# Soft mixture of experts: the weights are multiplied with gelu's vectors first, and with two experts' W2 after

## The reference

```python
dispatch = softmax(logits, over the rows n)                    # per slot
combine  = softmax(logits, over all 16 * 128 slots)            # per row
slot_in  = einsum('bnd,bnes->besd', x_ln, dispatch)
h        = gelu(einsum('besd,edh->besh', slot_in, W1) + b1)    # h: 128 slots x 64
slot_out = einsum('besh,ehd->besd', h, W2) + b2                # 128 slots x 256
out      = einsum('bsd,bns->bnd', slot_out, combine)
x        = layernorm(x + out)
```

## Time and profile before

| | us |
|---|---|
| median of 3 runs | 1168.07 (1167.62 to 1169.63) |
| profiled execution, its own time | 1169.36 |
| profiled execution, span of the core | 1167.6 |
| experts' stage in it, from the first `logits` at 813.8 | 353.8 |
| PE busy in the span | 1128.8 (97%) |

### The profile page before, as it was taken

How to read it: one execution, slowest core, us unless ns; L and a number is a source line. 1 busy time by engine, 2 the same in 40 slices (tenths; PEclk the granted TensorE clock), 3 DMA queues, 4 the chain that set the end, 5 groups by cost and what they waited for, 6 DMA issues and landing times. The chain is left out here.

```text
span 1167.6 us, 23652 instructions
## 1 busy us (share of the span) xinstructions
PE 1128.8 (97%) x8098; PEld 1039.1 (89%) x8098; DVE 803.1 (69%) x1896; ACT 798.5 (68%) x1696; POOL 717.0 (61%) x489
## 2 busy tenths in 40 slices
PE   7999999999999999999999999998989999999997
PEld 6899999999999999999999999998878889898886
DVE  5666776666677668666576766676586675777767
ACT  3766776666776667778677776664577895676565
POOL 5867767667775865777776676540176754556431
PEclk9899999999999999999999999999999999999999
DMA  3341211112111112111211111200110100110002
GB/s 113 86 132 37 50 33 46 33 36 57 45 29 33 47 43 49 47 33 28 51 42 46 33 46 37 50 7 6 37 33 19 42 19 15 37 24 24 10 10 73
DMA packets 49269, 47.84 MB, mean 41 GB/s; under 512 B 13176, under 2 KB 43384, under 8 KB 48896
## 3 DMA queue, kind: packets, MB, share of 16 engines
q1 hardware_dynamic: 48864, 46.25, 15.3%
q10 hardware_dynamic: 288, 0.07, 0.0%
HBM read 24.03 MB, written 2.10 MB: 22 GB/s over the span
## 5 line engine op out<-in xcount | busy, mean ns | idle before, releaser
L610 PE MATMUL ring<-kT,qT 128*128 128x512 f32 (+4 forms) x1056 | 238.6, 359 | 3.9 <-DVE kT L936 2.5
L794 ACT ACTIVATE exps<-ring,neg_max 128x128 f32<-128x128 f32 (+7 forms) x256 | 189.3, 742 | 54.8 <-DVE neg_max L947 53.0
L811 ACT ACTIVATE exp_parts<-turned 128x512 fp32r<-128x512 f32 x192 | 114.6, 597 | 125.5 <-PE turned L627 110.2
L610 PEld LDWEIGHTS ring<-kT,qT 128*128 128x128 f32 x1056 | 177.1, 191 | 15.0 <-DVE kT L936 2.9
L650 PE MATMUL mix<-exp_parts,v_parts 128*128 128x256 f32 x1152 | 183.8, 295 | 0.4 <-DVE exp_parts L965 0.4
L627 PE MATMUL turned<-ident,exps 128*128 128x128 f32 x1152 | 178.4, 273 | 1.2 <-ACT exps L794 0.6
L627 PEld LDWEIGHTS turned<-ident,exps 128*128 128x128 f32 x1152 | 141.6, 141 | 18.9 <-ACT exps L794 1.5
L965 DVE TENSOR_TENSOR exp_parts<-turned,exp_parts 128x512 fp32r<-128x512 f32 x192 | 131.9, 687 | 26.5 <-ACT exp_parts L811 26.1
L650 PEld LDWEIGHTS mix<-exp_parts,v_parts 128*128 128x128 f32 x1152 | 148.8, 189 | 0.6 <-DVE exp_parts L965 0.6
L1075 POOL TENSOR_TENSOR cos_part<-taken,cos_sb 128x1024 f32<-128x1024 f32 (+1 forms) x39 | 93.0, 2385 | 89.9 <-ACT taken L756 89.9
L947 DVE CUSTOM_DVE_ANT_1 ring<-ring,hidden 128x640 f32<-128x640 f32 (+3 forms) x128 | 131.5, 1027 | 14.9 <-PE ring L610 14.1
(11 more groups left out here) (249 smaller groups left out, 2270.0 us busy)
## 6 DMA issues: line engine op xcount, KB each, us to landing
rotated<-taken SPq DMA_DIRECT2D x76, 256.0 KB, 3.7
raw_q<-in_L_attn_Wq_dram SPq DMA_DIRECT2D x32, 128.0 KB, 3.6
raw_o<-in_L_attn_Wo_dram SPq DMA_DIRECT2D x32, 128.0 KB, 3.2
ffn_mu_next<-in_L_ffn_mu_dram SPq DMA_DIRECT2D x28, 128.0 KB, 2.5
y_sb<-in_L_attn_x_dram SPq DMA_DIRECT2D x4, 512.0 KB, 6.0
exps_and_mu<-in_L_ffn_mu_dram SPq DMA_DIRECT2D x1, 2048.0 KB, 8.5
ffn_w_sb<-in_L_ffn_W_dram SPq DMA_DIRECT2D x8, 256.0 KB
ffn_w_sb<-in_L_ffn_W_dram SPq DMA_DIRECT2D x14, 128.0 KB, 2.7
```

The lines of the kernel that those rows point to most:

```text
L610: last = nc.tensor.matmul(ring_cols(item, half * BANK, piece), qT[:, H % QUERIES, a, i * P:(i + 1) * P], kT[:, G % 2, m, half * piece:(hal ...
L794: nc.scalar.activation(dst, tile, ACT.Exp, bias=neg_max[:, H % 2, i:i + 1], scale=-1.0, accum_out=row_sum[:, H % 2, i:i + 1]).then_inc(don ...
L811: nc.scalar.activation(exp_parts[:, slot % HELD, 0, :], turned[:, n % 2, :], ACT.Copy).then_inc(done[kind], 1)
```

## The change

`output`, `slot_hi`, `slot_lo`, `weight_hi` and both `weight_lo` go, and so does the unsplit last unit. In their place, per unit v:
- `gelu` works on two experts at once (`hidden` is 128 = 2 x 64 partitions, 2 instructions in place of 4); `hidden_turn` transposes it (2 transposes, in `turned`), VectorE's `hidden_taken` copies it: 128 slots x 4 experts x 64.
- `mix` (v, half, n), a fill of `small`, sums over the slots for 512 rows (half 0 or 1) in plain f32. n = 0 and 1: two matmuls of 512 columns, 128 x 64 stationary, experts 2n and 2n+1 on the two column halves of the array. n = 2: four matmuls of 512 columns with a 128 x 32 stationary of ones, one expert on each column quarter, for the sums of the weights.
- `mix_hi` (ScalarE) and `mix_lo` (VectorE) split each result of 128 x 512: six of each per unit. `thin` in the plan is `mix`, `mix_hi`, `mix_lo` in this order.
- `w2_hi`, `w2_lo` split W2 once per unit, 128 x 512 (ScalarE, GpSimd); `b2_hi`, `b2_mixed` prepare b2 once.
- `spread` is 7 matmuls a tile: one of 258 columns with the sums, and 2 pairs of experts x 3 parts of 256 columns.
- `wide_inverse` becomes two f32 matmuls of 128 x 64, `gathered` one instruction in place of two.

The places in the list move too: `weight` 2 and 3 stand at the end of j = 1, after the folds; `spread` 0, 1, 2 of a unit stand in j = 2 behind all of its `mix`, and 3 to 7 in the next j = 0.

```diff
-        put(("slot_hi", v, pair), ("slot_lo", v, pair))
+    def thin(v, half, *parts):
+        for n in parts:
+            put(("mix", v, half, n), ("mix_hi", v, half, n), ("mix_lo", v, half, n))
...
-            if not unfolded:
-                slots(v, 1)
-            weight_parts(v, 0)
-            put(("weight", v, 2))
-            weight_parts(v, 1)
-            put(("weight", v, 3))
+            thin(v, 0, 0)
+            thin(v, 1, 0)
         if ripe and j == 2 and not last_unit:
-            weight_parts(v, 3)
-            if s == 10 and sequences > 1:
...
+        if ripe and j == 1 and not last_unit:
+            put(("weight", v, 2), ("weight", v, 3))
+        if last_unit and j == 2:
             spread(v, (0, 1))
         if s == total + 2 and sequences > 1:
...
             turn_units(1, (2, 3))
-        if j == 2:
+        if ripe and j == 2 and not last_unit:
+            thin(v, 1, 1, 2)
+            spread(v, (0, 1, 2))
+        if last_unit and j == 2:
             spread(v, (2, 3))
+        if j == 0 and ripe:
+            hidden_turned(v)
         if j == 0 and last_unit:
-            output(v)
-            put(("slot_last", v, 0), ("slot_last", v, 1))
-            put(*[("weight", v, k, half) for half in range(2) for k in range(4)])
+            put(*[("weight", v, k, 0) for k in range(4)])
         if j == 0:
             spread(v - 1, (6, 7))
-            if ripe and not last_unit:
-                put(("output", v, 0))
-                if not unfolded:
-                    put(("output", v, 1))
+        if j == 0 and last_unit:
+            thin(v, 0, 0)
+            put(("weight", v, 0, 1), ("weight", v, 1, 1))
+            thin(v, 0, 1)
+            put(("weight", v, 2, 1), ("weight", v, 3, 1))
+            thin(v, 0, 2)
+            thin(v, 1, 0, 1, 2)
...
+        if s == 4:
+            put(("b2_hi",), ("b2_mixed",))
+        if live and j == 1:
+            put(("w2_hi", u), ("w2_lo", u))
...
     STORED = {b: ((0, 4), (4, 6), (6, 8)) if b == B - 1 else ((0, 4), (4, 8)) for b in range(B)}
-    SMALL = ("gather", "fold", "output")
-    TURNED = ("turn", "turn_unit", "peaks", "wide", "wide_inverse")
...
                     for k in range(2):
-                        at_k = (2 * pair + k) % 4
-                        last = nc.tensor.transpose(turned_at_item(item)[:, k * S:(k + 1) * S],
-                                                   inv_total[:, at_k:at_k + 1].broadcast_to([P, P]), ident[:, :])
+                        at_k = 2 * pair % 4 + k
+                        last = nc.tensor.matmul(turned_at_item(item)[k * H:(k + 1) * H, 0:S],
+                                                inv_total[:, at_k:at_k + 1].broadcast_to([P, H]), ident[:, :], start=True, stop=True)
...
-                if kind == "output":
-                    v, pair = which
+                if kind == "hidden_turn":
+                    (v,) = which
                     pe.wait_ge(done["gelu"], v + 1)
-                    pe.wait_ge(bias_ones_ready, 1)
-                    pe.wait_ge(w2_loaded, (v + 1) * 32)
+                    free_turned(item)
+                    for pair in range(2):
+                        last = nc.tensor.transpose(turned_at_item(item)[:, pair * P:(pair + 1) * P], hidden[:, pair, :], ident[:, :])
+                    last.then_inc(done[kind], 1)
+                if kind == "mix":
+
+                    v, half, n = which
+                    ks = range(UNIT) if n == 2 else (2 * n, 2 * n + 1)
+                    for k in ks:
+                        if v == UNITS - 1:
+                            pe.wait_ge(done["weight"], count("weight", v, k, half))
+                        else:
+                            pe.wait_ge(done["weight"], count("weight", v, k))
+                    if n == 2:
+                        pe.wait_ge(done["b2_mixed"], 1)
+                    else:
+                        pe.wait_ge(done["hidden_taken"], v + 1)
                     free_small(item)
-                    for k in range(2):
-                        last = nc.tensor.matmul(small_at_item(item)[:, k * D:(k + 1) * D], hidden[0:H + 1, 2 * pair + k, :],
-                                                w2_sb[0:H + 1, 2 * pair + k, :], start=True, stop=True)
+                    for k in ks:
+                        if n == 2:
+                            last = nc.tensor.matmul(small_at_item(item)[32 * k:32 * k + 32, :], ones[:, :],
+                                                    kept(v, k)[:, half_cols(half)], start=True, stop=True)
+                        else:
+                            at_k = k % 2
+                            last = nc.tensor.matmul(small_at_item(item)[at_k * H:(at_k + 1) * H, :], hidden_slots[:, k * H:(k + 1) * H],
+                                                    kept(v, k)[:, half_cols(half)], start=True, stop=True)
                     last.then_inc(done[kind], 1)
...
-                        taken_by = "slot_last" if v == UNITS - 1 else "slot_lo"
-                        pe.wait_ge(done[taken_by], count(taken_by, v, 1))
-                        pe.wait_ge(slot_ones_ready, 3)
+                    pe.wait_ge(done["mix_lo"], thin_taken(v, 2 * t // TILES))
+                    pe.wait_ge(done["w2_lo"], v + 1)
                     if count(kind, *which) > 2:
                         pe.wait_ge(done["combine"], count(kind, *which) - 2)
-                    for k in range(UNIT):
-                        if v == UNITS - 1:
-                            if t in (0, TILES // 2):
-                                pe.wait_ge(done["weight"], count("weight", v, k, 2 * t // TILES))
-                            last = nc.tensor.matmul(spread_ps[:, t % 2, 0:WIDE], kept(v, k)[:, t * P:(t + 1) * P], slots_last[:, k, :],
-                                                    start=k == 0, stop=k == UNIT - 1)
-                            continue
-                        if t == 0:
-                            split = split_by(v, k)
-                            pe.wait_ge(done[split], count(split, v, k))
+                    out = spread_ps[:, t % 2, :]
+                    cols = slice(t * P, (t + 1) * P)
+                    nc.tensor.matmul(out[:, 0:WIDE], sums[:, cols], b2_parts[:, v % PER, :], start=True, stop=False)
+                    for pair in range(2):
                         for n, (a, m) in enumerate(PARTS):
-                            last = nc.tensor.matmul(spread_ps[:, t % 2, 0:WIDE], weights[:, a, k, t * P:(t + 1) * P], slots[:, m, k, :],
-                                                    start=k == 0 and n == 0, stop=k == UNIT - 1 and n == 2)
+                            last = nc.tensor.matmul(out[:, 0:D], thin_parts[:, a, pair, cols], w2_parts[:, v % 2, m, pair, :],
+                                                    start=False, stop=pair == 1 and n == 2)
                     last.then_inc(done[kind], 1)
...
                     nc.scalar.activation(kept(v, k)[:, cols], kept(v, k)[:, cols], ACT.Exp).then_inc(done[kind], 1)
-                if kind == "weight_hi":
-                    v, k = which
-                    act.wait_ge(done["weight"], count("weight", v, k))
+                if kind == "mix_hi":
+                    v, half, n = which
+                    act.wait_ge(done["mix"], count("mix", v, half, n))
                     if v:
-                        act.wait_ge(done["spread"], count("spread", v - 1, TILES - 1))
...
+                if kind == "mix_lo":
+                    v, half, n = which
+                    dve.wait_ge(done["mix_hi"], count("mix_hi", v, half, n))
+                    made = small_at_item(("mix", *which))
+                    if n == 2:
+                        nc.vector.scalar_tensor_tensor(sums[:, half_cols(half)], made, minus[:, 2:3], sums_hi[:, half_cols(half)].bitcast(F32),
+                                                       ALU.mult, ALU.add).then_inc(done[kind], 1)
+                    else:
+                        nc.vector.tensor_tensor(thin_parts[:, 1, n, half_cols(half)], made,
...
```

More of the change, by code:

```diff
@@ L1202, in plan_experts @@
         last_unit = v == units - 1
[L1203 removed]
         if changed:
[L1205 to L1207 removed]
+            spread(v - 1, (3, 4, 5))
         if live:
@@ L1391, in experts @@
     STORED = {b: ((0, 4), (4, 6), (6, 8)) if b == B - 1 else ((0, 4), (4, 8)) for b in range(B)}
-    SMALL = ("gather", "fold", "output")
-    TURNED = ("turn", "turn_unit", "peaks", "wide", "wide_inverse")
+    SMALL = ("gather", "fold", "mix")
+    TURNED = ("turn", "turn_unit", "peaks", "wide", "wide_inverse", "hidden_turn")
     small_fills = [item for item in plan if item[0] in SMALL]
@@ L1461, in kept, with thin_taken, thin_made, half_cols @@
             return (kept_1 if v % 2 else kept_0)[:, k, :]
-        def split_by(v, k):
-            return "weight_lo_a" if ("weight_lo_a", v, k) in at else "weight_lo_b"
+        def thin_taken(v, half):
+            return max(count("mix_lo", v, half, n) for n in range(3))
```

(4 more changed lines are left out.)

170 lines of the change are left out of this document (88 added, 82 removed).

## The result

The changed kernel takes 1256.73 us against 1168.28: a ratio of 1.075 (95% interval 1.0735 to 1.0765), 88 us slower. The profiled execution took 1257.12 with a span of 1255.3. One of the four executions behind this median ran at a granted clock of 0.555 and took 1878.79 us; the median of the other three is 1256.34. The forecast was 1231 with a range of 1203 to 1256, so the sign and most of the mechanism held, the size fell short by 26 us, and the time lies 0.7 us above the range (0.3 by the other three).

What follows compares the result with a forecast made beforehand. The tensor engine, at work for 97% of the span, was taken as the bound. New waits and work of 8.2 us a unit over seven units, adjusted to 56, plus 8 at the end, gave 1168 + 64 = 1231 us (rounded down), range 1203 to 1256.

Steps and rivals of the forecast that it cites:

- first step: j = 0, from the end of `logits`: 11.85 us against 11.17 before, +0.7, with `spread` 5 waiting 1.1 for `combine` 3.
- second and third up to `logits`: `mix` (0,1) waits 2.4 us for `weight` 3 behind the folds' copy; 14.2 us against 8.8 before, +5.4.
- third behind `logits`: `spread` 2 waits 2.7 us for `combine` 0; next `turn` at 8.2 us against 6.33 before, +1.9.
- fourth: Last step of a unit: as before, with two changes of column tiling, +0.2 us.
- the quarters: The 32-column `mix` matmuls, 16 records a unit: two at a time, 3.4 us; four at a time would give 1.7.
- The missed term: TensorE's clock in the new waits: a further loss if it left 1.00, with nothing put in the sum.
- TensorE's work: Tensor work per unit: 13.3 us removed, 14.8 added, so it grows by 1.5 us.
- Early units: Unit 1 costs +1 us, for no `spread` to give up and three b2 steps; units 3 and 7 about 1 less.
- The end: Last unit: six fills of `small` over two banks delay the first `combine` to 1155.6 from 1147.28, +8 us (5 to 10).
- Half of the waits: Rival: half of the 6.2 us of waiting per unit and some of the end go, 1204 us; chance 0.13.
- nothing overlaps: Rival: matmuls on column tiles run one at a time, 4.3 us more per unit, 1264 us; chance 0.08.
- Faster: Rival: tensor work alone decides, `weight` 3 and `combine` 0 come in time, no loss at the end, 1163 us; chance 0.04.

Runs made afterwards that it cites:

- the third move: Turning of the hidden vectors and its copy put ahead of tiles 3 to 5 and `run`, on the changed kernel with both other moves: 1197.7 us.
- the version at 1189.5: Tile 3 of `spread` put back in the next unit's first step, against the reordered kernel with weights 0 and 1 ahead of `exp` (1190.5 us): 1189.5 us, ratio 1.0181.

## Why the prediction was right, and where it was short

**The path by steps held.** Between the same points as in the prediction, unit 6 reads (forecast in brackets): first step 12.27 us (11.85), second and third up to `logits` 14.65 (14.2), third behind `logits` 8.50 (8.2), fourth 12.08 (11.3 from 11.06 + 0.2). Against before that is +1.1 (+0.7), +5.8 (+5.4), +2.2 (+1.9), +1.0 (+0.2): 10.1 instead of 8.2. Some of that nearness is luck: the measured steps hold 3.4 us of clock that the forecast had at nothing. Without it they come to +1.1, +4.1, +1.7 and -0.2, 6.7 in all, 1.5 below the forecast, of which the quarters are 0.9 and the first long wait 0.4. The waits were sized to some 0.5 us: 1.3 for 1.1, 2.0 for 2.4, 3.25 for 2.7. The experiments that took one of the two long waits away each (25 and 34 us less, and 59 with both and the third move) show that these waits, and what follows them, carry most of the 88 us. The argument for them was the order of each engine's list, and that was enough to find their places.

**The missed term is the clock.** The prediction said that it would be a further loss if it left 1.00, and put nothing in the sum. It left it: 57 us at half clock, at most 29 us of time, at least the 20 that the filled waits gave back. With the waits filled the kernel takes 1236.7, where the sum of waits and work was 1231. So the sum was about right for a TensorE that keeps its clock, in part because its errors cancel (the quarters and the early units below), and the range would have held with room if the term had been in. Put at nothing, it is the term that failed. In hindsight two waits in each of seven units at 1.7 us each, by the windows above, would have given 24 us; no row of the kernel before had this price. The count would have been luck as well: the trace has 14 such stretches between the two `turn`s, but three of them lie at the waits for `exp` and for the hidden vectors' copy in the first step, and in units 2 and 4 the 2.0 us wait is followed by none. The Trainium skill ("TensorE: Matmul & The Clock Gate", HAM oscillation — how this bites in real kernels) describes a loop that idles TensorE in every pass and pays for the clock in every pass, and reckons the loss as half of the time at the lower clock. The rows agree with the kind of loss and with the half, but the waits of the page's example are 3 to 5 us long; here the clock fell behind waits of 2.0 us as well, and not behind all of them, and the rows decide.

**Quarters run four at a time, not two.** Eight records of 512 columns in 1.07 us, with the change of mode, at a clock of 1.00 (1153.88 above), and 0.8 to 0.9 us for eight more of them. The Trainium skill ("TensorEngine Tiling (Array Packing)", Theoretical Speedup) gives up to four times for 32 columns, and these rows agree. The term was 0.9 us a unit too large, 6 us; it hid a part of the missing clock. The halves were taken rightly: four records in 1.08 us, two at a time. That half 1's quarters don't count was right.

**TensorE's work.** With four at a time it is 14.8 - 1.7 = 13.1 us a unit (both halves' quarters) against the 13.3 removed: -0.2 instead of +1.5. Unit 6 with the combines early, where the clock is 1.00 throughout, has TensorE busy for 40.76 us, against 40.55 in the earlier trace rows: +0.2. Over the whole page the version with the least waiting has TensorE busy for 1130.1 us, where the earlier trace rows has 1128.8. The change removes tensor work and adds as much; by TensorE's work alone it had nothing to gain, even with no new wait at all.

**Early units.** The prediction gave unit 1 one us more and had all others alike, but for units 3 and 7. By the distances between their first `turn`, units 1 to 4 grew by 15.4, 12.7, 10.4 and 12.4 us, and units 5 and 6 by 10.2 and 10.1. The wait of the second half of `turn` on the hidden vectors' copy, 0.4 us in unit 6, is 4.0, 2.9, 1.8 and 2.2 us long in units 1 to 4:
```profile
864.93 1.09 PE L1634 MATMUL ffn_turned<-ident,ffn_exps 128*128 128x128 f32 x4 [4.03 <-DVE ffn_hidden_slots L2052]
```
The copy stands behind `run` in VectorE's list, and that `run` took 3.37 us in unit 1. Unit 1 also had the clock at half for 10 us in a row. So the first step's wait was sized on unit 6 and was too small for these four; what makes it longer in units 3 and 4 was not tested. Unit 3, which was to be 1 us cheaper, is the cheapest of the first four; unit 7 isn't: up to its last `turn` it grew by 9.1 us, as unit 6 did over the same steps.

**The end.** +8 was forecast, and 43.8 - 35.8 = 8.0 measured; the first `combine` of the last unit comes at 1235.19, 87.9 us later than in the earlier trace rows, of which 79.7 were there at the `turn` of pair 31. Two errors cancel in it. The prediction's own terms, 1144.5 + 8.7, give 1153.2 for the last split, where it goes on with 1154.6; in the trace the six fills begin at 1225.31, 1.1 us later than forecast when the 79.7 are taken off, and end with the split at 1234.53, 9.2 us later. The small steps and the combine follow the last split at once, as in the prediction's chain:
```profile
1233.78 0.75 DVE L2058 SCALAR_TENSOR_TENSOR ffn_sums<-ffn_small,ffn_minus,ffn_sums_hi 128x512 fp32r<-128x512 f32 x1 [0.34 <-ACT ffn_sums_hi L1887]
1234.45 0.20 DVE L2117 RECIPROCAL ffn_inv<-ffn_mixed 128x8 f32<-128x8 f32 x1
...
1235.19 0.48 DVE L2099 SCALAR_TENSOR_TENSOR ffn_mixed<-ffn_mixed,ffn_fade,ffn_spread 128x258 f32<-128x258 f32 x1
```

**The rivals.** "Half of the waits" and "nothing overlaps" fell by the rows above. The second gave 1264, which is nearer to the measured time than the forecast is, but its mechanism isn't there: four records of the halves in 1.08 us, eight of the quarters in 1.07. "Faster" named its point rightly in one respect: with `weight` no longer behind the folds' copy that wait goes. But with both long waits gone the kernel is still at 1197.7, and at 1189.5 with further moves; none of the orders tried comes near the 1163 it gave. It counted on a shorter unit, on no loss at the end, and left out the small waits on `exp` and `combine` that come next (11.2 and 8.5 us in the version at 1189.5).

## What to carry to other kernels

Where TensorE runs without gaps, an edit that makes it wait for another engine costs the wait and often a stretch at half clock on whatever matmuls follow; take both into the sum, the second as a range, and try idle matmuls in the wait to learn which part is the clock. Before costing the matmuls that are saved, walk the lists of the engines that feed them: two weights placed earlier in ScalarE's list were worth 25 us here, and two tiles with their combines placed earlier in TensorE's and VectorE's lists 34. Narrow column tiles do run side by side, but the halves and quarters in plain f32 added to TensorE what the smaller `spread` and the missing `output` saved.

## What the runs showed of the hardware

The clock behind a wait depends on more than that wait: 2.0 us idle was followed by a clock of 0.51 in units 5 and 6 of the changed kernel, by 1.00 in its units 2 and 4, and by 1.00 in unit 6 when only the 3.25 us waits were taken away. With idle matmuls of 128 columns in four of the waits (10 to 24 in each, 2.13 us for 18) it was 1.00 in every unit.

VectorE's `run` takes 1.23 us, and 3.20 in the steps where GpSimd subtracts the peaks meanwhile, in the changed kernel; in unit 6 of the kernel before it is 1.23 and 3.02, so this is no part of the 88 us. First VectorE's rows in the changed kernel, then GpSimd's beside the second:
```profile
1156.97 1.23 DVE L1998 TENSOR_TENSOR ffn_run<-ffn_run,ffn_kept 128x1024 f32<-128x1024 f32 x1 [2.51 <-ACT ffn_kept L1852]
...
1174.44 3.20 DVE L1998 TENSOR_TENSOR ffn_run<-ffn_run,exps_and_mu 128x1024 f32<-128x1024 f32 x1
```
```profile
1171.81 10.42 POOL L2178 TENSOR_TENSOR ffn_kept<-ffn_kept,ffn_peak_wide 128x1024 f32<-128x1024 f32 x4 [7.63 <-ACT ffn_peak_wide L1874]
```
It delays `top`, and with it `exp`, in the first step of a unit, and the version at 1189.5 us still waits 1.0 to 2.9 us for `exp` there in units 1 to 4. The Trainium skill ("SBUF — State Buffer", SBUF: two separate sides) says that a VectorE instruction with two SBUF inputs and a GpSimd one that reads SBUF lock each other out of a shared port pair for a whole instruction. `run` has two such inputs, and the 3.20 us agree with it: its own 1.23 and the 2 us of a subtraction that had begun (2.40 us each, one of the four 3.36). No run here took one of the two away.
